# Four small reorderings in an attention and scan kernel: head loads and maxima on SyncE, the maxima's way out of PSUM, VectorE's order over the PSUM ring, and the two projection halves

## The chip, the cores and the metric

The kernel runs on one core of a Trainium2 chip. The metric is the device time of one execution in microseconds. The kernel before takes 8861.15 us, the median of 3 runs (8851.8 to 8868.71).

## What is computed

The input x has shape (8, 32, 32, 192). Four layers follow one another, each added to its input after a group norm without parameters (`_gn`, 32 groups over the image):

```
x = x + L0(_gn(x))   # A: attention, 12 heads of 16 over 1024 tokens, rope on q and k
x = x + L1(_gn(x))   # B: depthwise 3x3 convolution and a selective scan in 4 directions
x = x + L2(_gn(x))   # C: attention with relative position bias rel_h + rel_w
x = x + L3(_gn(x))   # D: neighbourhood attention, window 7x7, no bias
attn = softmax(q @ k * scale (+ bias)); out = (attn @ v) @ proj (+ b)
```

## The kernel before

The kernel calls the layers A, B, C, D. B (`scan_*`) is a stage of its own. A, C and D share the functions `attn_tensor`, `attn_scalar`, `attn_vector`, `attn_pool` and `attn_sync`, one program for each engine (PE, ACT, DVE, POOL and SP, which issues all DMAs). Each engine works strictly in the order of its program, and they meet at semaphores.

**Turns.** A layer is a row of turns n. A turn does one step of scores and one step of weights, `LEAD` turns apart. A head takes `STEPS` turns, 8 in A and C (one 128-row tile against 1024 keys each) and 4 in D (two tiles of 320 keys each). So an image of 12 heads has 96 turns in A and C and 48 in D, and the lead is 13, 13 and 8.

- `scores(n)`: PE multiplies a query tile with all keys; DVE takes the row maximum (L927) into `mx`.
- `maxima(h)`: after a head's last scores PE transposes `mx` (L681). DVE's `negated` reads the transposed 8x128 tile from PSUM and splits -max into two fp32r parts in D (`nm`, L936, L938) and three bf16 parts in A and C (`nb`, L941 to L947). SP copies them as extra rows into the head's queries (`maxima` in `attn_sync`, L1100), so that the second product comes out with the maximum subtracted. These rows serve the first weights unit of that head.
- `weights(g)`: PE multiplies a key tile with all queries (L694, L698, L700), and ACT takes the exponential (L825) into `pt`.
- `values`: PE multiplies `pt` with v into `px` (L724); ACT and DVE take it out (`outputs`, L832, L954) into `os`; SP's `store` moves it to `dn` and `ocm` (L1115, L1118).

**The ring.** All PSUM results but values go through a ring of 3 slots of 1024 columns. `ring(L)` lists the units in PE's order: in a turn first the planned ones ("sums", "job", "rot", "tokens", "proj"), then the relatives (C alone), scores, maxima, weights. Unit i has slot i % 3. `claim` makes PE wait until unit i - 3 has been read. A maxima unit counts as read when `negated` has ended (`a.nm`).

**The plan.** `agenda(L)` puts the rest of the work at fixed turns: the norm's statistics and sums, four jobs for each image (projections to q and k in halves of 96 channels, with the split into parts, L768 to L903 and SP's `part`, L1065), rot and turn (rope, A alone), tokens (v), the reciprocals of the sums and their spreading (`back`, L1123, `spread`, L1134, POOL's `normal`), the two halves of the output projection (`proj`; PE L631, DVE `residual`, L970, L972) and "leave" (store the image, load the one after next, L388, L382). The two proj halves of an image stand in successive turns, leave one turn later. In D these are turns 20, 21 and 22 of the next image.

**Loads.** A head's q and k parts come from DRAM into one of 4 buffers (`load` in `attn_sync`, L1088, 384 KB a head). For k, a part is read with a repeated (broadcast) outer dimension. In D the load of head h + 3 is issued in the first turn of head h, as seen from scores, and needed in the first turn of the next head. It waits for the parts in DRAM (`s.stored`) and until the buffer's last weights step has run (`s.st_ps`). In that turn of D SP does the planned work, then `maxima`, then `load`; `store` of a head comes two turns later.

**DVE's turn** is scores(n) first, then the planned work in plan order, then relatives, negated, outputs.

Of the kernel before, what the change touches and what calls it, by code (L numbers as in the profile page):

```python
# [7 lines left out]
F32 = mybir.dt.float32  # L8
F32R = mybir.dt.float32r
BF16 = mybir.dt.bfloat16  # L10
ALU = mybir.AluOpType
# [3 lines left out]
B, H, W, C = 8, 32, 32, 192  # L15
N = H * W
NH, HD = 12, 16
CP = 96
NC = C // CP
# [109 lines left out]
class HeadSignals:  # L129
    def __init__(self, sem):  # L130
        self.qk_ps = sem("qk_ps")
        self.top = sem("top")
        self.low = sem("low")
        self.v_ps = sem("v_ps")
        self.v_used = sem("v_used")
        self.mt = sem("mt")
        self.nm = sem("nm")
        self.odd = sem("odd")
        self.os = sem("os")
        self.o_in = [sem(f"o_in{i}") for i in range(2)]  # L140
        self.rdn = sem("rdn")
        self.rd_out = sem("rd_out")
        self.rb_in = sem("rb_in")
        self.oc = [sem(f"oc{i}") for i in range(NC)]
        self.proj_ps = sem("proj_ps")
# [219 lines left out]
def turns(L, img):  # L365

    return B * LAYERS.index(L) + img
# [39 lines left out]
def norm_variance(nc, dve, m, sums, turn):  # L407
    dve.wait_ge(m.i.stat_sums, turn + 1)
    nc.vector.tensor_copy(m.gs[:], sums.rearrange("p (c s) -> p c s", c=NC)).then_inc(m.i.sums_used, 1)
    nc.vector.drain()  # L410
    nc.vector.tensor_tensor(m.gt[:], m.gs[:, :, 0], m.gs[:, :, 0], ALU.mult)
    nc.vector.drain()
    nc.vector.tensor_tensor(m.gv[:], m.gs[:, :, 1], m.gt[:], ALU.subtract).then_inc(m.i.var, 1)
# [52 lines left out]
def agenda(L):  # L466

    plan = {}

    def put(n, kind, img, i=0):  # L470
        plan.setdefault(n, []).append((kind, img, i))

    size, lead = per_image(L), LEAD[L]
    ahead, behind = AHEAD[L], BEHIND[L]
    for img in range(B):
        start = size * (img - 1)
        for c in range(NC):
            put(start + ahead["norm"] + c, "statistics", img, c)
        put(start + ahead["norm"] + 1, "moments", img)
        put(start + ahead["norm"] + 3, "sums", img)  # L480
        put(start + ahead["norm"] + 4, "apply", img)
        for i, n in enumerate(ahead["jobs"]):
            for kind, lag in JOB_LAGS[L].items():
                put(start + n + lag, kind, img, i)
        for i, n in enumerate(ahead["tokens"]):
            put(start + n, "tokens", img, i)
        for c, end in ((0, size * img + lead + 7 * STEPS[L] - behind["reciprocal"]), (1, size * (img + 1))):
            for kind in ("reciprocal", "back", "spread", "normal"):
                put(end + behind[kind], kind, img, c)
        for c in range(NC):  # L490
            put(size * (img + 1) + behind["proj"] + c, "proj", img, c)
        put(size * (img + 1) + behind["proj"] + 2, "leave", img)
    return plan


def turns_of(L, plan):

    return range(min(plan), max(plan) + 1)
# [18 lines left out]
def maxima_ready(L, n):  # L517

    return n % STEPS[L] == 0 and 0 < n <= per_image(L) * B
# [31 lines left out]
def attn_tensor(nc, pe, m, L):  # L551
# [8 lines left out]
    def claim(unit):  # L560

        i = place[unit]
        if i >= SLOTS:
            old = units[i - SLOTS]
            if old[0] == "scores":
                pe.wait_ge(s.mx_used, old[1] + 1)
            elif old[0] == "weights":
                pe.wait_ge(s.pt, old[1] + 1)
            elif old[0] == "maxima":
                pe.wait_ge(a.nm, heads + old[1] + 1)  # L570
            elif old[0] == "relative":
                pe.wait_ge(s.rq, 2 * old[1] + old[2] + 1)
            elif old[0] == "sums":
                pe.wait_ge(m.i.sums_used, turns(L, old[1]) + 1)
            elif old[0] == "tokens":
                pe.wait_ge(a.v_used, 2 * (images + old[1]) + old[2] + 1)
            elif old[0] == "rot":
                pe.wait_ge(s.turned, 4 * old[1] + old[2] + 1)
            elif old[0] == "proj":
                pe.wait_ge(m.i.x_done, NC * turns(L, old[1]) + old[2] + 1)  # L580
            elif L == "A":
                pe.wait_ge(s.raw, 4 * old[1] + old[2] + 1)
            elif L == "C":
                pe.wait_ge(s.rest, 4 * old[1] + old[2] + 1)
            else:
                pe.wait_ge(a.low, 4 * (images + old[1]) + old[2] + 1)
        return m.ring[:, i % SLOTS, :]
# [267 lines left out]
def attn_vector(nc, dve, m, L):  # L855
# [14 lines left out]

    def turn(img, i):

        dve.wait_ge(s.rot_ps, 4 * img + i + 1)
        nc.vector.tensor_tensor(m.rs[:], m.ring[0:CP, slot[("rot", img, i)], :], m.sin[:], ALU.mult) \
            .then_inc(s.turned, 1)
# [53 lines left out]
    def negated(h):  # L929

        dve.wait_ge(a.mt, heads + h + 1)
        if h >= 1:
            dve.wait_ge(s.nm_in, MAX_IN[L] * h)
        mt = m.ring[0:NT, slot[("maxima", h)], 0:P]
        if L == "D":
            nc.vector.tensor_scalar(m.nm[:, 0, :], mt, -1.0, None, ALU.mult)  # L936
            nc.vector.drain()
            nc.vector.scalar_tensor_tensor(m.nm[:, 1, :], mt, -1.0, m.nm[:, 0, :].bitcast(F32),  # L938
                                           ALU.mult, ALU.subtract).then_inc(a.nm, 1)
        else:  # L940
            nc.vector.tensor_scalar(m.nb[:, 0, :], mt, -1.0, None, ALU.mult)  # L941
            nc.vector.drain()
            nc.vector.scalar_tensor_tensor(m.nr[:], mt, -1.0, m.nb[:, 0, :], ALU.mult, ALU.subtract)
            nc.vector.drain()
            nc.vector.tensor_copy(m.nb[:, 1, :], m.nr[:])
            nc.vector.drain()
            nc.vector.tensor_tensor(m.nb[:, 2, :], m.nr[:], m.nb[:, 1, :], ALU.subtract).then_inc(a.nm, 1)  # L947
# [24 lines left out]
            nc.vector.tensor_tensor(x, psum, x, ALU.add).then_inc(m.i.x_done, 1)  # L972

    for n in turns_of(L, plan):
        if 0 <= n < total:
            scores(n)
        for kind, img, i in plan.get(n, []):
            if kind == "statistics":
                if i == 0:
                    dve.wait_ge(m.i.x_in, 16 * (turns(L, img) + 1))  # L980
                norm_statistics(nc, m, m.x[img % 2], i)
            if kind == "moments":
                norm_moments(nc, m, turns(L, img))
            if kind == "sums":
                norm_variance(nc, dve, m, m.ring[0:CP, slot[(kind, img, i)], 0:2 * NC], turns(L, img))
            if kind == "apply":
                if img:
                    dve.wait_ge(a.v_ps, 2 * (images + img))
                norm_apply(nc, dve, m, m.x[img % 2], turns(L, img))
            if kind == "turn":  # L990
                turn(img, i)
            if kind == "sum":
                total_of(img, i)
            if kind == "rest":
                rest(img, i)
            if kind == "low":
                low(img, i)
            if kind == "reciprocal":
                reciprocal(img, i)
            if kind == "proj":  # L1000
                residual(img, i)
        for h, axis in relatives(L, n):
            relative(h, axis)
        if maxima_ready(L, n):
            negated(n // steps - 1)
        g = n - lead
        if g % steps == 2 and steps < g <= total + 2:
            outputs(g // steps - 1)
# [31 lines left out]
def attn_sync(nc, sp, m, L, x_from, x_to, d):  # L1040
    s, a = m.s[L], m.a
# [95 lines left out]
    for n in turns_of(L, plan):  # L1137
        for kind, img, i in plan.get(n, []):
            if kind == "part":
                part(img, i)  # L1140
                jobs += 1
                if img == 0 and i == 1:
                    for h in range(NBUF):
                        load(h, jobs)
            if kind == "back":
                back(img, i)
            if kind == "spread":
                spread(img, i)
            if kind == "leave":
                store_image(sp, m, L, img, x_to)  # L1150
                if img + 2 < B:
                    load_image(sp, m, L, img + 2, x_from)
        if maxima_ready(L, n):
            maxima(n // steps - 1)
        h, left = divmod(n - lead, steps)
        if left == 0 and 1 <= h and h - 1 + NBUF < NH * B:
            sp.wait_ge(s.st_ps, steps * h)
            load(h - 1 + NBUF, jobs)
        if left == 2 and 1 <= h <= NH * B:
            store(h - 1)  # L1160

# [579 lines left out]
```

## Time and profile before

| | before |
|---|---|
| median of 3 runs | 8861.15 us |
| profiled execution | 8870.59 us |
| its span | 8868.8 us |
| PE busy | 7117.3 us, 80% |
| DVE busy | 5281.6 us, 60% |
| ACT busy | 3280.4 us, 37% |
| granted TensorE clock, mean | 0.864 |
| stage A / B / C / D, about | 50 to 1880 / 4562 / 7410 / 8869 us |

Times within the profile are microseconds from the start of the span. A clock of 1.00 is TensorE at 2.4 GHz, 0.50 at 1.2 GHz. "PE" is the matmul, "PEld" the weight load, "SPq" what SP's sequencer issues. An arrow `<-` in a wait names who released it. L numbers are lines of the kernel before. The profiled execution is 9.4 us over the median of the runs.

### The profile page before, as it was taken

Reading aid. Unit: us, or ns where it says so; the run is one execution under the profiler, and the core shown is the slowest. Engines: PE = TensorE matmul, PEld = TensorE weight load, DVE = VectorE, ACT = ScalarE, POOL = GpSimd, SP = SyncE. Lnnn points to the kernel's source line nnn. Section 1 sums busy time; section 2 is a strip of 40 time slices with the busy share of each in tenths; the row PEclk is TensorE's granted clock in tenths of the full one; section 3 lists DMA queues with packets and bytes.
Section 4 is the critical chain, followed back from the end, with each engine's and each line's share of the span. In section 5 each row is a group of like instructions: output and inputs, shape, how many; then the busy total and the mean of one; then the engine's idle time right before and its main releaser. Section 6 shows DMA issues by size and latency. Waiting matters only on the chain. (4 is left out here: it accounts for less than half of the span.)

```text
span 8868.8 us, 86314 instructions
## 1 busy us (share of the span) xinstructions
PE 7117.3 (80%) x32664; PEld 2841.9 (32%) x32664; DVE 5281.6 (60%) x5310; ACT 3280.4 (37%) x3610; POOL 1168.2 (13%) x468
## 2 busy tenths in 40 slices
PE   6888888867777777777779999999989996777776
PEld 2222222223223223233234343344333432333332
DVE  5777777757777767777765555555555553333333
ACT  2555555532323322322323343333433432222222
POOL 0000000014334334334320000000000000000000
PEclk9999999988878778778778999999989997888787
DMA  2111111100000000000001001111010101222221
GB/s 65 47 46 48 48 48 48 46 23 0 7 7 0 7 7 0 7 7 0 4 29 29 27 29 35 29 30 30 27 35 27 30 25 54 65 66 62 64 68 46
DMA packets 152812, 282.83 MB, mean 32 GB/s; under 512 B 46858, under 2 KB 53762, under 8 KB 152398
## 3 DMA queue, kind: packets, MB, share of 16 engines
q1 hardware_dynamic: 152398, 277.31, 10.8%
q8 instruction: 260, 4.26, 0.2%
q14 instruction: 154, 1.26, 0.0%
HBM read 165.34 MB, written 89.79 MB: 29 GB/s over the span
## 5 line engine op out<-in xcount | busy, mean ns | idle before, releaser
L927 DVE TENSOR_REDUCE mx<-ring 128x1 f32<-128x1024 f32 (+1 forms) x1920 | 2187.8, 1141 | 2536.0 <-PE ring L674 1255.0
L825 ACT ACTIVATE pt<-ring 128x1024 f32<-128x1024 f32 (+1 forms) x1920 | 1868.4, 981 | 2836.0 <-PE ring L700 1329.5
L724 PE MATMUL px<-pt,vo 128*32 128x512 f32 (+3 forms) x8064 | 1277.2, 616 | 9.5 <-ACT pt L825 9.3
L671 PE MATMUL ring<-kb,qb 96*128 96x512 bf16 x3072 | 1121.2, 407 | 203.0 <-DVE rq L912 96.2
L698 PE MATMUL ring<-qb,kb 99*128 99x512 bf16 x3072 | 1124.0, 408 | 161.7 <-DVE nb L947 67.9
L1533 POOL TENSOR_TENSOR hc<-hs,crep 128x1024 f32<-128x1024 f32 x384 | 979.7, 2551 | 1684.0 <-DVE hs L1489 1593.7
L1228 PE MATMUL ring<-duh,spread 96*128 96x512 f32 x1536 | 650.7, 537 | 362.0 <-DVE hs L1478 230.5
L1489 DVE TENSOR_TENSOR_SCAN hs<-ring,hs 128x1024 f32<-128x1024 f32 x384 | 874.5, 2277 | 2.1 <-ACT ring L1376 2.1
L700 PE MATMUL ring<-rq,hot 128*128 128x512 f32 x1536 | 865.5, 622 | 0.0
L674 PE MATMUL ring<-hot,rq 128*128 128x512 f32 x1536 | 856.6, 616 | 0.0
L1376 ACT ACTIVATE ring<-ring,arow 128x1024 f32<-128x1024 f32 x384 | 415.9, 1083 | 947.8 <-PE ring L1217 947.8
L698 PEld LDWEIGHTS ring<-qb,kb 99*128 99x128 bf16 x3072 | 266.7, 100 | 1319.9 <-issue 684.5
L1478 DVE TENSOR_TENSOR hs<-ring,brep 128x1024 f32<-128x1024 f32 x384 | 467.3, 1217 | 358.8 <-PE ring L1228 312.6
L671 PEld LDWEIGHTS ring<-kb,qb 96*128 96x128 bf16 x3072 | 280.7, 100 | 907.0 <-issue 396.5
L1217 PE MATMUL ring<-dth,spread 96*128 96x512 f32 x1536 | 521.1, 467 | 30.4 <-DVE hs L1489 29.6
L667 PE MATMUL ring<-ks,qs 112*128 112x320 f32 x768 | 270.4, 441 | 330.5 <-DMA ks<-qk_split 295.2
L1228 PEld LDWEIGHTS ring<-duh,spread 96*128 96x128 f32 x1536 | 307.3, 218 | 699.8 <-DVE hs L1478 298.8
L1243 PE MATMUL px<-hc,fold 128*32 128x512 f32 x1536 | 476.0, 1018 | 31.8 <-POOL hc L1533 30.9
L1217 PEld LDWEIGHTS ring<-dth,spread 96*128 96x128 f32 x1536 | 313.4, 221 | 480.6 <-issue 346.4
L1030 POOL TENSOR_TENSOR ocn<-ocm,rb 96x1024 f32<-96x1024 f32 x24 | 56.7, 2362 | 2717.1 <-DMA rb<-reciprocals 2388.0
L1030 POOL TENSOR_TENSOR ocm<-ocm,rb 96x1024 f32<-96x1024 f32 x24 | 56.4, 2351 | 2428.2 <-DMA rb<-reciprocals 2428.2
L667 PEld LDWEIGHTS ring<-ks,qs 112*128 112x128 f32 x768 | 147.2, 234 | 609.5 <-issue 505.4
(169 smaller groups left out, 6792.5 us busy)
## 6 DMA issues: line engine op xcount, KB each, us to landing
qk_parts<-part SPq DMA_DIRECT2D x192, 192.0 KB, 2.4
qb<-qk_parts SPq DMA_DIRECT2D x192, 96.0 KB
kb<-qk_parts SPq DMA_DIRECT2D x192, 96.0 KB
ocm<-os SPq DMA_DIRECT2D x576, 32.0 KB
rb<-reciprocals SPq DMA_DIRECT2D x288, 64.0 KB, 2.5
qb<-qk_parts SPq DMA_DIRECT2D x192, 64.0 KB
kb<-qk_parts SPq DMA_DIRECT2D x192, 64.0 KB
qk_split<-hi SPq DMA_DIRECT2D x32, 384.0 KB, 3.5
```

What stands on the lines that cost most here:

```text
L671: last = nc.tensor.matmul(out[:, half], m.qb[u][0:BR, q], m.kb[u][0:BR, half], start=True, stop=L == "A")
L674: last = nc.tensor.matmul(out[:, half], m.rq[u][:, q], m.hot[:, half], start=False, stop=True)
L698: last = nc.tensor.matmul(out[:, half], m.kb[u][:, k], m.qb[u][:, half], start=True, stop=L == "A")
L700: last = nc.tensor.matmul(out[:, half], m.hot[:, k], m.rq[u][:, half], start=False, stop=True)
L724: last = nc.tensor.matmul(m.px[32 * g:32 * g + 32, h % 2, lo - f * HF:hi - f * HF], m.vo[img % 2][:, t, VW * head:VW * head + VC], pt[:, l ...
L825: nc.scalar.activation(pt, ps, ACT.Exp, scale=1.0 if L == "C" else HD ** -0.5).then_inc(s.pt, 1)
L927: nc.vector.tensor_reduce(out, ps, AX.X, ALU.max).then_inc(s.mx_used, 1)
L1217: last = nc.tensor.matmul(m.s2[:, i % 2, f * HF:(f + 1) * HF], m.spread[:, ORDER[j], :], m.dth[k % 2][:, part, f * HF:(f + 1) * HF], start ...
L1228: last = nc.tensor.matmul(m.s1[:, f, :], m.spread[:, ORDER[j], :], m.duh[k % 2][:, part, f * HF:(f + 1) * HF], start=part == 0, stop=part ...
L1243: last = nc.tensor.matmul(m.px[32 * band:32 * (band + 1), f, :], m.fold[:, v, :], rhs, start=False, stop=t >= TILES - BANDS, skip_group_ch ...
L1489: nc.vector.tensor_tensor_scan(m.hs[i % HSS][:], m.s2[:, i % 2, :], m.hs[i % HSS][:], 0.0, ALU.mult, ALU.add).then_inc(s.h, 1)
L1533: nc.gpsimd.tensor_tensor(m.hc[i % HCS][:], m.hs[i % HSS][:], m.crep[k % 2][:], ALU.mult).then_inc(s.hc, 1)
```

## The change

- In `attn_sync`, `load` comes before `maxima` within a turn.
- `negated` takes the transposed maxima out of PSUM with its first operation, into `nr`, and signals `mt_used`; the parts are then made from `nr`. PE's claim after a maxima unit waits for `mt_used`. D has three operations instead of two, A and C five instead of four.
- DVE does the plan's "sums", "turn", "proj", "rest" (in C) and "low" (in D) ahead of scores(n), in PE's order. `turn` also waits for the sum of the job before.
- The second proj half stands two turns after the first, and leave one turn later than before (three after the first half).

```diff
+        self.mt_used = sem("mt_used")
...
         for c in range(NC):
-            put(size * (img + 1) + behind["proj"] + c, "proj", img, c)
-        put(size * (img + 1) + behind["proj"] + 2, "leave", img)
+            put(size * (img + 1) + behind["proj"] + 2 * c, "proj", img, c)
+        put(size * (img + 1) + behind["proj"] + 3, "leave", img)
...
             elif old[0] == "maxima":
-                pe.wait_ge(a.nm, heads + old[1] + 1)
+                pe.wait_ge(a.mt_used, heads + old[1] + 1)
...
     def turn(img, i):
+        if 4 * img + i:
+            dve.wait_ge(s.rotated, 4 * img + i)
         dve.wait_ge(s.rot_ps, 4 * img + i + 1)
...
         mt = m.ring[0:NT, slot[("maxima", h)], 0:P]
+        nc.vector.tensor_scalar(m.nr[:], mt, -1.0, None, ALU.mult).then_inc(a.mt_used, 1)
+        nc.vector.drain()
         if L == "D":
-            nc.vector.tensor_scalar(m.nm[:, 0, :], mt, -1.0, None, ALU.mult)
+            nc.vector.tensor_copy(m.nm[:, 0, :], m.nr[:])
             nc.vector.drain()
-            nc.vector.scalar_tensor_tensor(m.nm[:, 1, :], mt, -1.0, m.nm[:, 0, :].bitcast(F32),
-                                           ALU.mult, ALU.subtract).then_inc(a.nm, 1)
+            nc.vector.tensor_tensor(m.nm[:, 1, :], m.nr[:], m.nm[:, 0, :].bitcast(F32), ALU.subtract).then_inc(a.nm, 1)
         else:
-            nc.vector.tensor_scalar(m.nb[:, 0, :], mt, -1.0, None, ALU.mult)
+            nc.vector.tensor_copy(m.nb[:, 0, :], m.nr[:])
             nc.vector.drain()
-            nc.vector.scalar_tensor_tensor(m.nr[:], mt, -1.0, m.nb[:, 0, :], ALU.mult, ALU.subtract)
+            nc.vector.tensor_tensor(m.nr[:], m.nr[:], m.nb[:, 0, :], ALU.subtract)
...
     for n in turns_of(L, plan):
+        for kind, img, i in plan.get(n, []):
+            if kind == "sums":
+                norm_variance(...)
+            if kind == "turn":
+                turn(img, i)
+            if kind == "rest" and L == "C":
+                rest(img, i)
+            if kind == "low" and L == "D":
+                low(img, i)
+            if kind == "proj":
+                residual(img, i)
         if 0 <= n < total:
             scores(n)
         for kind, img, i in plan.get(n, []):
...
-            if kind == "rest":
+            if kind == "rest" and L == "A":
                 rest(img, i)
-            if kind == "low":
+            if kind == "low" and L != "D":
                 low(img, i)
...
# attn_sync
-        if maxima_ready(L, n):
-            maxima(n // steps - 1)
         h, left = divmod(n - lead, steps)
         if left == 0 and 1 <= h and h - 1 + NBUF < NH * B:
             sp.wait_ge(s.st_ps, steps * h)
             load(h - 1 + NBUF, jobs)
+        if maxima_ready(L, n):
+            maxima(n // steps - 1)
         if left == 2 and 1 <= h <= NH * B:
             store(h - 1)
```

## Rows read from the trace of the kernel before

**Rows 1.** Stages A, C, D: length, busy PE, PEld, DVE, ACT, POOL; clock; DMA; GB/s.

```profile
50.00:1880.00 1830.00, 1541.75 (x7024) 438.96 (x7024) 1295.96 (x1514) 941.68 (x1008) 112.72 (x48) 0.94 0.16 46
...
4562.00:7410.00 2848.00, 2563.73 (x16112) 1123.85 (x16112) 1479.03 (x1646) 1110.29 (x1168) 37.81 (x16) 0.91 0.10 30
7410.00:8868.80 1458.80, 1051.79 (x4208) 472.40 (x4208) 530.23 (x842) 415.11 (x560) 37.78 (x16) 0.79 0.22 64
```

**Rows 2.** PE's waits in stage D: releaser, us in total, times, longest.

```profile
PE ring L667 <- DMA ks<-qk_split: 295.2, 67, 8.1
...
PE ring L694 <- DVE x L972: 12.8, 7, 1.8
```

**Rows 3.** The timeline of one plain head in D: start, us, engine, operation.

```profile
7802.12 0.53 PE L667 MATMUL ring<-ks,qs 112*128 112x320 f32 x2 [3.03 <-DMA ks<-qk_split]
...
7804.08 1.38 SPq L1100 DMA_DIRECT2D qs<-nm  x2
...
7805.57 1.11 SPq L1088 DMA_DIRECT2D qs<-qk_split  x2
...
7806.90 0.56 PE L667 MATMUL ring<-ks,qs 112*128 112x320 f32 x2
...
7808.94 1.29 SPq L1115 DMA_DIRECT2D dn<-os  x2
...
7810.28 1.18 SPq L1118 DMA_DIRECT2D ocm<-os  x2
7814.15 0.87 PE L667 MATMUL ring<-ks,qs 112*128 112x320 f32 x2 [3.95 <-DMA ks<-qk_split]
```

**Rows 4.** The waits of SP's queue in stage D.

```profile
SPq L1100 <- DVE nm L938: 390.0, 75, 11.7
...
SPq L1134 <- DMA reciprocals<-rdn: 50.9, 16, 6.0
...
SPq L381 <- DMA out<-x: 23.8, 6, 4.0
```

**Rows 5.** The timeline of a head in D that starts without a stall.

```profile
7871.20 0.56 PE L667 MATMUL ring<-ks,qs 112*128 112x320 f32 x2
...
7875.88 0.67 DVE L954 TENSOR_TENSOR os<-px,odd 64x512 f32<-64x512 f32 x1
...
7876.14 0.56 PE L667 MATMUL ring<-ks,qs 112*128 112x320 f32 x2
```

**Rows 6.** Two half-microsecond windows of the plain head, columns as in rows 1.

```profile
7803.50:7804.00 0.50, 0.50 (x4) 0.00 (x0) 0.43 (x3) 0.50 (x1) 0.00 (x0) 0.50 0.00 0
...
7810.50:7811.00 0.50, 0.00 (x0) 0.00 (x0) 0.00 (x0) 0.00 (x0) 0.00 (x0) 1.00 0.15 59
```

**Rows 7.** PE's waits in stage A.

```profile
PE ring L698 <- DVE nb L947: 62.0, 84, 2.1
...
PE ring L671 <- DVE rs L874: 27.6, 21, 2.7
...
PE ring L671 <- DVE gs L409: 4.1, 7, 0.9
```

**Rows 8.** PE's waits in stage C.

```profile
PE ring L698 <- DVE raw L891: 20.4, 14, 1.5
...
PE ring L671 <- DVE x L970: 4.3, 7, 0.6
```

**Rows 9.** The timeline of a job's reading in C.

```profile
5459.67 1.11 ACT L768 ACTIVATE part<-ring,qk_bC 96x1024 bf16<-96x1024 f32 x1 [2.47 <-PE ring L597]
...
5461.65 1.27 DVE L891 SCALAR_TENSOR_TENSOR raw<-ring,qk_bC,part 96x1024 f32<-96x1024 f32 x1
...
5462.98 0.39 PE L698 MATMUL ring<-qb,kb 99*128 99x512 bf16 x1 [1.40 <-DVE raw L891]
```

**Rows 10.** The timeline of the maxima in A.

```profile
1006.72 0.27 DVE L941 TENSOR_SCALAR nb<-ring 8x128 bf16<-8x128 f32 x1
...
1008.04 0.60 PE L698 MATMUL ring<-qb,kb 99*128 99x512 bf16 x2 [0.58 <-DVE nb L947]
```

More of the change, by code:

```diff
@@ L974, in attn_vector @@
     for n in turns_of(L, plan):
+        for kind, img, i in plan.get(n, []):
+            if kind == "sums":
+                norm_variance(nc, dve, m, m.ring[0:CP, slot[(kind, img, i)], 0:2 * NC], turns(L, img))
+            if kind == "turn":
[6 more added lines that the diff above has]
+                residual(img, i)
         if 0 <= n < total:
@@ L983, in attn_vector @@
                 norm_moments(nc, m, turns(L, img))
-            if kind == "sums":
-                norm_variance(nc, dve, m, m.ring[0:CP, slot[(kind, img, i)], 0:2 * NC], turns(L, img))
             if kind == "apply":
@@ L989, in attn_vector @@
                 norm_apply(nc, dve, m, m.x[img % 2], turns(L, img))
-            if kind == "turn":
-                turn(img, i)
             if kind == "sum":
                 total_of(img, i)
-            if kind == "rest":
+            if kind == "rest" and L == "A":
                 rest(img, i)
-            if kind == "low":
+            if kind == "low" and L != "D":
                 low(img, i)
@@ L999, in attn_vector @@
                 reciprocal(img, i)
-            if kind == "proj":
-                residual(img, i)
         for h, axis in relatives(L, n):
```

## The prediction

> **What bounds the kernel now.** I read the span by stages first, then who waited for whom in each, then the order of time around the longest wait.
>
> The stage table [rows 1] shows TensorE (PE) busy for 84% of stage A, 90% of C and 72% of D, while DVE is at 71%, 52% and 36%. PE sets the pace in all three, and its idle time is what this change can reach: 288 us in A, 284 us in C, 407 us in D. Stage B is not touched. The low clock is a second cost: the granted clock averages 0.79 in D against 0.91 and 0.94.
>
> In D one wait stands out [rows 2]: 67 times PE waits for a head's qs/ks rows, 295.2 us in all, 4.4 us each.
>
> Why those rows are late is seen in the order of time around one plain head [rows 3]. Its first scores start at 7802.12. The SP queue, which issues all DMAs, stands until the DVE has the negated maxima, issues them at 7804.08 (1.38 us), and only then issues the load at 7805.57. The load's user starts at 7814.15. So a load takes 8.6 us from first issue to use, and the period is 3.5 + 8.6 = 12.0 us. SP had been free since the previous store; the queue's own waits [rows 4] put 390.0 us, 75 times, on "DVE nm".
>
> PE alone doesn't need 12 us: a head that starts without a wait has its first, and its fourth turn 4.94 us later [rows 5], so its four turns take 4.94 + 1.61 = 6.55 us, at full clock. After the 4 us of a stall the clock is granted at half, 1.2 GHz [rows 6], and the first two turns take 4.8 us instead of 3.3 [rows 3, 5].
>
> In A and C the waits are short ones for ring slots [rows 7, 8]. In A: 62.0 us for the maxima's slot (84 times), and five rows for slots of rot, proj and sums, from 27.6 to 4.1, together 74.1 us. In C, beside the relatives' slots, which the change leaves alone: six rows for job, proj, sums and maxima, from 20.4 down to 4.3, together 65.5 us.
>
> **The load ahead of the maxima.** In A and C a load's turn is 5 modulo 8 and the maxima's is 0, so the swap changes nothing there. In D both fall on n % 4 = 0. The load's only other waits are for its parts in DRAM and for st_ps of the turn before, which PE has passed when the head starts. It is then issued as soon as the store of turn n - 2 is out of SP's queue.
>
> The new chain: in a full-clock head, os starts 4.68 us and ends 5.35 us after the head's start [rows 5]; dn and ocm take SP 1.29 + 1.18 us, with gaps 2.5 us [rows 3]; so SP is free at 7.9 us. The load issued then is used 8.6 us later, at 16.5 us, and its user is the head after next. So the period is 16.5 / 2 = 8.3 us, 1.7 us over PE's 6.55. The stall doesn't vanish, it falls from 4.4 to about 1.7 us. If each stall still brings the half clock for two turns (+1.5 us, os later by up to 1.5 us) the period is 9.6 us. I take 8.8.
>
> Sum for D: 67 waits x (4.4 - 1.7) = 181 us. Clock: 1.5 us x 67 = 100 us if all of it came back; half, 50 us, since 1.7 us of idleness stays in each head. Together 231 us. Checked by the period: 67 x (12.0 - 8.8) = 214 us. Ends: PE alone, 67 x (12.0 - 6.55) = 365 us; and 80 us, where the stall still costs 3.2 us a head because the maxima or SP's queue are late in the load's place.
>
> What moves behind the load: the maxima's two issues. SP has them out 2.3 us (four load issues) + 1.4 us after the load's start. They are needed one scores unit after the load is, since both serve turn n + 4. But they sit behind 384 KB. The trace shows what this means. Between 7810.5 and 7811.0 the DMA share is 0.15 with 59 GB/s moved [rows 6]: the tail of the load is on two of 16 engines, for some 4 us. And a small DMA (reciprocals, 24 KB) issued behind a load kept the queue waiting for up to 6.0 us [rows 4]. So the maxima land with the load's tail, not before it. I cost that at nothing: cover is that weights come after scores and the transpose, 0.6 us. Without cover it is that lateness, 67 times.
>
> By the Trainium skill ("DMA: Bandwidth & Descriptors", Queues, rings and completion order; and on how many engines) a DMA is split over the largest k up to 16 that divides its slowest dimension, always on the lowest-numbered engines, and each engine takes descriptors in ring order. The ks load with its broadcast outer 2 would be on engines 0 and 1 and the 8-row maxima on 0 to 7, so the maxima would stand behind the load on two engines. By that rule the trace's two busy engines agree, and it makes the first rival below.
>
> **Leave one turn later, proj two units apart.** Image stores and loads (SP, plan turn 22 of 48 in D) move to turn 23. SP stands some 4.0 us for the image's store before it issues the next load [rows 4], now directly ahead of the head load of turn 24, and the 768 KB image load is now directly ahead of it in the DMA queues; before, a store and the maxima lay between. Once per image, about 3 us: 8 x 3 = -24 us in D. In A and C loads have slack (PE waited for kb once in each, at the start), nothing. The spacing itself removes the DVE's two residuals back to back; with the reorder D's proj waits go, 12.8 us [rows 2] and a second row of half that. Net in D about 231 - 24 + 19 = 226, rounded to 225 us.
>
> **DVE in ring order.** PE fills plan units before scores(n), but DVE reduced scores(n) first. In C [rows 9] a job's part is ready at 5460.78 (5459.67 + 1.11), DVE does the reduction of 1.23 us first, then rest, and PE's weights start at 5462.98, 1.40 us late. After: rest 5460.8 to 5462.1, weights 0.9 us earlier; scores(n)'s reduction ends at 5463.3 instead of 5461.7, and scores(n + 1) may wait 0.3 us for it. Such a stall goes by two thirds. proj and sums go whole, since their data is ready when PE ends. The relatives keep their place after scores(n), so their waits stay. C: 65.5 us x 0.75 = 50 us (20 to 90, the upper end with clock regained after the 2 us stalls).
> In A the same: 74.1 us. DVE is the busier engine there, and each operation that comes first makes scores(n) later by 1.2 us, which the next weights unit claims. Half: 37 us. The wait for s.rotated that turn gains is for DVE's own sum of two turns earlier; nothing. In D low can't start before ACT's hi, which ends when the reduction does: nothing.
>
> **Maxima by one operation.** In A the slot was held by four operations from 1006.72 on, and PE's weights started at 1008.04, 0.58 us late [rows 10]. Now it is free after the first, 0.27 us. But the chain is one operation longer, a cast of 0.21 us and a drain of 0.07 to 0.13: the two reductions that stand behind it end 0.3 us later, and the third weights unit after the maxima claims the second one's slot. By the rows it then starts only 0.1 us earlier, though units after it can regain 0.3. I take 0.25 of 0.58: 96 x 0.25 = 24 us (-20 to 60). C and D have slack on DVE: nothing but the 5.9 us counted above. The nm for SP is 0.3 us later, and SP has the load to issue in that time.
>
> **Sum.** D 225, C 50, A 37 + 24 = 61: 336 us. The profiled execution took 8870.6 us (span 8868.8): 8870.6 - 336 = 8534.6. The median shown is 9.4 us under the profiled one: 8525.
>
> **Rivals.**
> 1. PE waits in D for the maxima or for SP's queue in the load's place. For: [rows 4, 6]. Against: the load itself ends at the same moment. If the maxima land 2 us after it, D gives 67 x 2 = 134 us less: 91 + 111 = 202 us, 8660.
> 2. A and C give nothing, as DVE turns each freed slot into a late reduction. For: A's two reductions back to back behind the maxima; against: C's DVE idles half the time. D alone: 8861 - 225 = 8636.
> 3. Slower: the maxima come so late behind the load that they set D's period. Place: weights of turn n + 4; they also hold DVE, whose next negated waits for nm_in. From 12.0 - 8.3 = 3.7 us behind the load D gains nothing; at 3.7 + 111 / 67 = 5.4 us the whole is even; at 8 us it is 8861 + 67 x 4.3 - 111 = 9038. Against: behind the last load descriptor only 4 KB per row remain.
> 4. The clock comes back in full and stalls shrink with it (PE near 6.9 us a head): D 340, C 70, A 61: 8390 or so.
>
> Chances: the forecast 0.62, rival 1 0.11, rival 2 0.14, rival 4 0.10, rival 3 0.03. The range, 8430 to 8690, takes in rivals 1 and 2 and half of 4. What a measurement can tell from no change is 0.2%, 18 us. Faster than that 0.95, within it 0.02, slower 0.03.
>
> **What would show it.** In the changed profile: in D, heads without jobs 8.3 to 9.6 us apart, the ks wait near 1.7 us a time, "DVE nm" as SP's wait cut to a fraction, and D's clock above 0.85 (if it stays at 0.79, the clock half fails). No wait for "nb" in A's PE rows, but some for "mx". C's waits for rq as before, those for raw, x and gs under 20 us. Wrong would be: a PE wait for qs<-nm in dozens (rival 1), A's 61 us missing (rival 2), or D's heads still over 11 us apart.

## The result and the profile after

The changed kernel takes 8531.05 us, the median of 4 runs (8513.62 to 8533.49), against 8864.93 us for the kernel before on the same chip: ratio 0.9624, 95% interval 0.961 to 0.9638. Forecast was 8525, in the range 8430 to 8690. The profiled execution has a span of 8531.7 us. The sum was right by luck: two errors cancel in it.

The stage table after, first A, C and D, columns as in [rows 1] (B, between A and C, is 2680 us in both):

```profile
40.00:1770.00 1730.00, 1513.85 (x7024) 425.02 (x7024) 1313.84 (x1617) 942.59 (x1008) 113.03 (x48) 0.97 0.17 49
...
4453.00:7226.00 2773.00, 2531.36 (x16112) 1127.13 (x16112) 1496.46 (x1742) 1110.40 (x1168) 37.97 (x16) 0.92 0.11 31
7226.00:8531.70 1305.70, 983.37 (x4208) 446.19 (x4208) 546.30 (x938) 415.29 (x560) 37.73 (x16) 0.84 0.24 71
```

Taken between the first image loads of the stages, the change by stage is:

```
          before    after   measured   forecast
A         1839.5   1730.0    -109.5       -61
B         2681.3   2680.4      -0.9         0
C         2848.3   2773.4     -74.9       -50
D         1456.4   1305.5    -150.9      -225
```

PE's waits after, in A, where [rows 7] stood:

```profile
PE ring L672 <- ACT pt L826: 35.0, 140, 0.3
PE ring L699 <- DMA qb<-nb: 21.6, 13, 2.6
PE ring L682 <- DVE mx L930: 18.5, 23, 1.3
PE ring L672 <- DVE mx L930: 14.6, 10, 8.2
...
PE ring L699 <- DVE mx L930: 12.0, 19, 1.1
PE ring L672 <- DVE x L974: 7.1, 14, 0.5
...
PE ring L699 <- DVE nr L938: 6.1, 10, 0.7
```

The rows for mx in A before:

```profile
PE ring L671 <- DVE mx L927: 12.3, 8, 7.1
...
PE ring L681 <- DVE mx L927: 11.4, 9, 1.3
...
PE ring L698 <- DVE mx L927: 3.5, 8, 1.3
```

In C the two long rows for the relatives, before:

```profile
PE ring L671 <- DVE rq L912: 96.2, 77, 2.5
PE ring L648 <- DVE rq L912: 54.7, 78, 1.7
```

After, in C, where [rows 8] stood, then in D, where [rows 2] stood:

```profile
PE ring L672 <- DVE rq L915: 113.2, 84, 2.5
PE ring L649 <- DVE rq L915: 60.9, 79, 1.7
...
PE ring L699 <- DVE raw L894: 4.0, 7, 0.6
```

```profile
PE ring L668 <- DMA ks<-qk_split: 226.4, 49, 13.5
PE ring L668 <- DVE lo L902: 21.2, 21, 1.0
...
PE ring L695 <- DVE nr L938: 0.9, 3, 0.4
PE ring L695 <- DVE x L976: 0.2, 1, 0.2
```

What the reader is to see: the maxima's 62.0 us in A (was nb) is 6.1 us for nr. The five rows for rot, proj and sums, 74.1 us, are down to 7.1 us for x, but the rows for mx grew from 27.2 to 45.1 us. C's 20.4 us for raw is 4.0, while the relatives' rows (all that wait for rq) grew from 177.5 to 196.2 us. D has 49 ks waits instead of 67, but they are longer, 4.6 us a time and up to 13.5. Counted by the head that they stand ahead of, 16 of the 67 waits and 106 of the 295 us were those of heads 7 and 10 of an image; now these are 16 of the 49, and 129 of the 226 us. Among the plain heads the wait ahead of heads 1 and 3 is gone (but for the first image), and the one ahead of heads 0 and 2 is 2.2 to 4.0 us. SP's queue in D, where [rows 4] stood:

```profile
SPq L1124 <- DVE os L958: 184.7, 66, 8.6
SPq L1109 <- DVE nm L943: 169.1, 49, 11.7
...
SPq L1082 <- DMA qk_split<-lo: 29.6, 8, 4.3
...
SPq L382 <- DMA out<-x: 24.4, 6, 4.4
```

"DVE nm" fell from 390.0 to 169.1 us. The wait for the parts just written (qk_split<-lo) is 29.6 us, and was less than half of that before:

```profile
SPq L1073 <- DMA qk_split<-lo: 12.9, 8, 3.6
```

Two plain heads of D after, where [rows 3] stood:

```profile
7888.52 1.13 SPq L1097 DMA_DIRECT2D qs<-qk_split  x2
...
7890.45 0.53 PE L668 MATMUL ring<-ks,qs 112*128 112x320 f32 x2 [3.32 <-DMA ks<-qk_split]
...
7897.29 1.28 SPq L1124 DMA_DIRECT2D dn<-os  x2
...
7898.47 0.55 PE L668 MATMUL ring<-ks,qs 112*128 112x320 f32 x2
...
7899.91 1.62 SPq L1097 DMA_DIRECT2D qs<-qk_split  x2
...
7908.56 0.87 PE L668 MATMUL ring<-ks,qs 112*128 112x320 f32 x2 [3.48 <-DMA ks<-qk_split]
```

The load is issued when the store's issues end, is used 8.6 us later (7899.91 to 7908.56), and the two heads together take 18.1 us: one of 8.0 without a stall, one of 10.1 with one. The forecast chain said 8.3 to 9.6 us a head.

The whole of D and A, head by head, shows what each part does. Each number is the time from a head's first scores to the next one's, mean of images 1 to 6, worked out from the starts of the scores matmuls; s1 to s4 are the four parts alone on the kernel before, u, v and w variants of the changed kernel (below). A plain head is one without planned work:

```
D, head        0    1    2    3    4    5    6    7    8    9   10   11   sum
before       12.6 12.2 12.3 12.3 15.7 17.0 14.1 16.4 17.8 20.0 13.3 12.2  175.9
s1 load       8.3  9.9  8.8  9.9 14.6 16.2 13.9 16.3 17.7 19.9 13.3 10.3  159.2
s2 one op    12.7 12.4 12.4 12.6 15.5 17.1 14.1 15.6 17.0 19.9 13.4 12.4  175.2
s3 order     12.3 12.0 12.2 12.2 15.6 14.5 13.7 16.0 16.4 19.9 14.2 12.1  171.2
s4 spacing   12.4 11.9 12.2 12.0 15.4 15.4 18.3 16.6 16.9 19.9 13.7 12.0  176.8
after         8.0 10.1  9.3  9.8 14.5 12.1 19.2 14.7 17.8 20.0 14.2 10.0  159.7
u2 image      8.4  9.9  8.1  9.9 14.5 11.3 15.2 19.1 17.9 19.8 13.2  9.8  157.1
u3 parts      8.4  9.9  8.7  9.7 14.8 11.6 19.1 15.6 17.5 17.9 14.3  9.8  157.4
u5 16 rows    6.9  7.3  7.4  7.4 11.6 11.0 15.0 16.1 17.7 15.8 12.8  7.1  136.2
u6 maxima    12.5 12.5 12.4 12.4 15.3 12.4 17.9 16.6 17.0 20.0 14.2 12.5  175.7
w1 no spac.   8.2 10.1  8.2 10.0 14.6 11.5 13.1 16.6 17.3 19.9 13.5  9.8  152.9
v3           7.2  7.3  7.2  7.3 11.4 11.3  6.6 22.5 17.6 14.6 11.7  7.1  131.8
A, head
before       13.9 13.9 13.9 24.9 14.8 22.4 26.4 26.3 21.7 17.6 13.9 13.9  223.5
s2 one op    13.4 13.4 13.5 26.6 14.6 22.6 26.4 26.5 19.2 16.6 13.5 13.4  219.8
s3 order     13.9 13.9 13.9 22.8 14.1 20.2 22.9 25.6 18.6 16.4 13.9 13.9  209.8
after        13.4 13.4 13.4 20.0 17.7 21.0 22.8 25.4 17.3 16.7 13.4 13.5  207.9
```

### The profile page after: what moved, and what is told of

Its sections match the earlier page's. It is cut to its first block and busy times, and to the rows that moved or that the text cites. A ratio compares the mean times of both kernels' runs of the same rounds, so it can differ in the third digit from the quotient of the medians.

```text
span 8531.7 us, 86921 instructions
## 1 busy us (share of the span) xinstructions
PE 6989.7 (82%) x32664; PEld 2806.6 (33%) x32664; DVE 5325.8 (62%) x5598; ACT 3281.8 (38%) x3610; POOL 1169.1 (14%) x468
## 5 line engine op out<-in xcount | busy, mean ns | idle before, releaser
L725 PE MATMUL px<-pt,vo 128*32 128x512 f32 (+3 forms) x8064 | 1232.0, 599 | 7.6 <-ACT pt L826 7.5
L699 PE MATMUL ring<-qb,kb 99*128 99x512 bf16 x3072 | 1102.0, 400 | 49.6 <-DMA qb<-nb 21.6
L668 PE MATMUL ring<-ks,qs 112*128 112x320 f32 x768 | 255.4, 420 | 255.2 <-DMA ks<-qk_split 226.4
L675 PEld LDWEIGHTS ring<-hot,rq 128*128 128x128 f32 x1536 | 327.1, 213 | 10.9 <-issue 10.3
```

Of the source, the lines that this page charges most:

```text
L675: last = nc.tensor.matmul(out[:, half], m.rq[u][:, q], m.hot[:, half], start=False, stop=True)
L699: last = nc.tensor.matmul(out[:, half], m.kb[u][:, k], m.qb[u][:, half], start=True, stop=L == "A")
L725: last = nc.tensor.matmul(m.px[32 * g:32 * g + 32, h % 2, lo - f * HF:hi - f * HF], m.vo[img % 2][:, t, VW * head:VW * head + VC], pt[:, l ...
```

## The experiments

All ratios are to the kernel before on the same chip. Stage times are those of one profile each; B, which no kernel here touches, lies between 2668 and 2682 us in them, so a difference under 10 us says nothing.

Totals and stage times don't quite agree. The profile of the kernel before is of an execution of 8870.59 us, while its median was 8839.0 to 8844.7 us on the chips of all experiments. So stage differences to it add up to some 26 to 32 us more than the totals give, and which stage holds them is not shown. D is hardly the place: s2, which does nothing for D's pace, has D at 1451.8 us on another chip, against 1456.4.

### The four parts, each alone

**s1, the load first.** The two lines go from ahead of SP's head load to behind it.

```diff
-        if maxima_ready(L, n):
-            maxima(n // steps - 1)
...
+        if maxima_ready(L, n):
+            maxima(n // steps - 1)
```

> The kernel before with the head load ahead of the maxima alone. My theory: only D moves. Stage D falls from 1456 us to about 1300, heads without planned work 8.0 to 10 us apart; A stays at 1839 within 5 us, C at 2848, B at 2681. Total about -150 us, ratio 0.983. Rival (part of D's gain came from VectorE's order and the early slot): D falls by under 110 us here.

8724.28 us, ratio 0.9868 (0.9848 to 0.9887). D 1304.0 us, C 2844.9, A 1849.7. The gain is in D, -152 us, nearly all of it in the heads without planned work (12.3 to 8.3 and 9.9 us); heads 4 and 5 give 1.9 us an image, heads 6 to 10 don't move. The total gives less, 117 us (100 to 135). By D's stage time, on which it was stated, the rival is out. The two terms of the forecast can be read apart here. The ks waits fell from 295.2 us by 97:

```profile
PE ring L667 <- DMA ks<-qk_split: 198.2, 48, 7.8
```

And PE's busy time in D fell from 1051.79 us by 55, for the same 4208 matmuls:

```profile
7420.00:8724.00 1304.00, 996.60 (x4208) 451.41 (x4208) 530.05 (x842) 414.67 (x560) 37.78 (x16) 0.83 0.24 71
```

Together that is the 152 us.

**s2, the maxima by one operation** (the `negated` and `mt_used` lines of the diff above).

> The kernel before with the maxima taken out of PSUM by one operation alone. My theory: A gains 0.5 us for each of 96 heads, so about -48 us, C -6, D 0 (the load sets its pace): ratio 0.994. Rival, the forecast's own pricing (DVE's longer chain takes half back): A -24 us, ratio 0.997.

8820.85 us, ratio 0.9979 (0.997 to 0.9989). A 1807.1 us (-32), its plain heads 13.9 to 13.4 us; C 2837.0, D 1451.8. The plain heads give the 0.5 us that I expected, twice the forecast's 0.25, but head 3 gives 1.7 back. In A the wait for the maxima's slot fell from 62.0 to 3.9 us and the stage by 32 only: the waits for qb<-nb rose from 12.1 to 20.9 us and PE's busy time by 9. The total gives 19 us (10 to 27), nearer to the rival's 24 than to my 54.

**s3, DVE in ring order** (the `attn_vector` loop and `turn` of the diff above).

> The kernel before with VectorE's new order alone. My theory: A and C gain in the heads with jobs alone, A -35 to -50 us, C -50 us, D within 15 us: ratio 0.989. Rival (the reductions that now stand behind the planned work take it all back): within 20 us of before.

8670.73 us, ratio 0.9815 (0.98 to 0.9829): the largest part. A 1745.2 us (-94), C 2799.1 (-49), D 1414.1 (-42). I was too low in A and missed D. The stage table of A and D in it has the clock up in both:

```profile
40.00:1785.00 1745.00, 1503.27 (x7024) 430.49 (x7024) 1298.33 (x1520) 940.64 (x1008) 112.96 (x48) 0.97 0.16 49
...
7257.00:8670.70 1413.70, 1037.61 (x4208) 466.43 (x4208) 526.55 (x842) 414.76 (x560) 37.72 (x16) 0.81 0.22 66
```

In A the granted clock rises from 0.94 to 0.97 and PE's busy time falls by 38 us, though it does the same matmuls; its idle time between the same marks falls by 47. The slot waits [rows 7] are worth 74 us by themselves, so a part of them came back as other waits: the rows for mx are 36.8 us instead of 27.2, and x has 3.6. s1, s2 and s4 have 0.94 to 0.95 still, so the clock came with this part. The total gives 164 us (152 to 177) where the three stages give 185.

**s4, the projection halves two turns apart** (the two `put` lines).

> The kernel before with the two projection halves two turns apart and leave one turn later, alone. My theory: A -10 to -20 us, C -15 us, D +5 to +20 us since the image's store and load now stand ahead of a head load: ratio 0.997. Rival (spacing is worth nothing once it stands alone, because DVE still reduces scores first): all stages within 5 us.

8867.74 us, ratio 1.0035 (1.0022 to 1.0048): slower by a third of a per cent. Per image, A and C are even: A's heads 3 and 4 take 40.9 us together instead of 39.7. In D head 6 goes from 14.1 to 18.3 us and head 5 from 17.0 to 15.4. Spacing alone buys nothing. By stage nothing is lost either (A 1840.6, C 2843.6, D 1455.7 us), and this profile is of its fastest execution, so where the third of a per cent goes is not shown.

### Parts taken out of the changed kernel

**u6, the maxima first again** (s1's edit reversed).

> The changed kernel, with the maxima ahead of the head load again. My theory: A and C as in the changed kernel (1730 and 2773 us), D between 1400 and 1425 us, where VectorE's order alone left it: ratio 0.974 to 0.978. Rival (the load's place is worth less once the other three parts are in, since D then waits for leave and parts): D under 1370 us, ratio under 0.971.

8680.06 us, ratio 0.9816 (0.9801 to 0.9831). D 1451.0 us, A 1730.4, C 2780.3. So the load's place is worth 145.5 us in D with the other parts in, as alone; both numbers I gave were off, because D stands at 1451 without it and not at 1414. Head 6 has most of that, 17.9 us against 13.7 in s3, which has no spacing. The plain heads show a part too: 12.5 us against 12.2 in s3, since with the maxima first the longer chain (0.3 us) stands ahead of the load. The ratios of u6 and the changed kernel are 170 us apart, so more than D shows.

**w1, the halves in successive turns** (leave again in the turn after the second half).

```diff
-            put(size * (img + 1) + behind["proj"] + 2 * c, "proj", img, c)
-        put(size * (img + 1) + behind["proj"] + 3, "leave", img)
+            put(size * (img + 1) + behind["proj"] + c, "proj", img, c)
+        put(size * (img + 1) + behind["proj"] + 2, "leave", img)
```

> The changed kernel with the two projection halves in successive turns and leave one turn later, as before: the first three parts of the change alone. My theory (spacing is worth nothing in A and C and delays the head load behind the image load in D): D's heads 5 and 6 fall from 31.3 to about 28 us, A and C within 8 us, total 20 to 30 us under the changed kernel; ratio 0.960. Rival (with VectorE in ring order the spacing pays, since DVE's residual and reduction no longer stand back to back): 10 us or more over the changed kernel.

8483.6 us, ratio 0.9596 (0.9582 to 0.961). D 1257.5 us, 48 under the changed kernel, A and C within 4 us of it. Head 6 of D goes from 19.2 to 13.1 us. So the fourth part costs 48 us by D's profile. The totals say less: 25 us between the ratios, and 39 against u4, which is the changed kernel but for the maxima's chain and ran on the same chip. The forecast's 24 is at the low end. Without the spacing the parts simply add up in D: 1456.4 less the 152.4 of s1, the 4.6 of s2 and the 42.3 of s3 is 1257.1 us. Why the spacing is worth nothing in D alone (s4) and costs 48 us here is shown in part only: it costs head 6 of an image 4.2 us there and 6.1 here, and the 1.6 us that it gave back in head 5 there it does not give here (11.5 us in w1, 12.1 in the changed kernel).

**u4, the slot released by the second operation** of the old, shorter chain.

```diff
-        nc.vector.tensor_scalar(m.nr[:], mt, -1.0, None, ALU.mult).then_inc(a.mt_used, 1)
-        nc.vector.drain()
...
+            nc.vector.tensor_scalar(m.nb[:, 0, :], mt, -1.0, None, ALU.mult)
+            nc.vector.drain()
+            nc.vector.scalar_tensor_tensor(m.nr[:], mt, -1.0, m.nb[:, 0, :], ALU.mult, ALU.subtract) \
+                .then_inc(a.mt_used, 1)
```

> The changed kernel with the old, shorter maxima chain (four operations in A and C, two in D); the ring slot is released after the second operation, the last that reads PSUM. My theory (in A's plain heads the slot's release is what counted and the longer chain costs nothing there; in D the chain stands ahead of SP's maxima only): A's plain heads stay at 13.4 us within 0.1, D within 10 us of the changed kernel's 1305; total within 15 us of it, ratio 0.962 to 0.964. Rival (DVE is short in A and the extra operation costs what the early slot gives): A's plain heads at 13.1 or less, A by 25 us or more.

8522.17 us, ratio 0.9637 (0.9618 to 0.9656), the changed kernel's within the interval. A's plain heads stay at 13.4 us, A 1730.6, D 1301.7. So the early release was the gain. A release 0.3 us later and a chain one operation shorter move it no further together; that neither would alone is not shown, since the two could offset each other.

### What holds D now

Head 6 of the changed kernel in order of time:

```profile
7953.40 1.29 SPq L1124 DMA_DIRECT2D dn<-os  x2
...
7954.74 1.18 SPq L1127 DMA_DIRECT2D ocm<-os  x2
...
7955.96 0.57 SPq L389 DMA_DIRECT2D out<-x  x1
...
7960.63 0.32 SPq L383 DMA_DIRECT2D x<-x_C  x1
7961.07 1.14 SPq L1097 DMA_DIRECT2D qs<-qk_split  x2
...
7972.84 0.87 PE L668 MATMUL ring<-ks,qs 112*128 112x320 f32 x2 [12.04 <-DMA ks<-qk_split]
```

SP puts the head's store first, then the image's store, stands 4 us, issues the image load and then the head load. That one is used 11.8 us after its issue instead of 8.6, and PE stands 12.04 us. The same load, the one for head 7, in four kernels, from the starts of SP's issues and of the scores matmul, images 1 to 6:

```
             image load ahead by    issue to use
before              4.4             8.4 to 8.7
w1 no spac.         3.0             8.6 to 10.1
s4 spacing          1.9             9.6 to 10.5
after               0.4            11.5 to 12.9
```

The image's store moves nearer too, from 8.8 us ahead of the head load to 5.0 to 5.6, so the table doesn't tell the two apart.

**u2, the image load behind the head load** in D. It is noted in the queue's turn and issued behind the head load and the maxima.

```diff
             if kind == "leave":
                 store_image(sp, m, L, img, x_to)
-                if img + 2 < B:
+                if L == "D":
+                    coming = img + 2
+                elif img + 2 < B:
                     load_image(sp, m, L, img + 2, x_from)
...
+            if coming < B:
+                load_image(sp, m, L, coming, x_from)
+            coming = B
```

> The changed kernel, with D's image load issued after the next turn's head load and maxima instead of ahead of them. My theory (head 6 of an image takes 19.2 us instead of 14.1 because SP stands for the image's store and then puts 768 KB ahead of the head load): the head load's issue to use falls from 11.7 back to 8.6 us, head 6 to 15 to 16 us, D by 20 to 30 us; ratio to before 0.960. Rival (the 19.2 us come from SP's wait for the store alone, not from the order in the DMA queues): head 6 stays over 18 us.

8513.04 us, ratio 0.9629 (0.9615 to 0.9643); the total can't tell it from the changed kernel. D 1284.8 us in the profile. Head 6 falls to 15.2 us, but not for my reason. The same place in this run:

```profile
7935.73 0.57 SPq L389 DMA_DIRECT2D out<-x  x1
7936.42 2.45 SPq L1097 DMA_DIRECT2D qs<-qk_split  x2
...
7948.83 0.87 PE L668 MATMUL ring<-ks,qs 112*128 112x320 f32 x2 [8.27 <-DMA ks<-qk_split]
```

From issue to use the load takes 12.4 us here, and 12.4 to 13.2 in images 1 to 6: it did not fall. What fell away is the 4 us for which SP stood between the image's store and the head load; the load is issued 0.7 us behind the store instead of 5.1, and the store's 768 KB now stand where the image load's stood. Head 7 rises from 14.7 to 19.1 us. 2.9 of these 4.4 us are PE's busy time, 13.5 to 16.4 us for the same matmuls, at a granted clock of 0.58 instead of 0.76 (mean of images 1 to 6). And DVE, whose statistics need the image, waits longer for it, first in the changed kernel, then here:

```profile
DVE gn L395 <- DMA x<-x_C: 42.2, 7, 7.8
```

```profile
DVE gn L395 <- DMA x<-x_C: 64.8, 7, 11.0
```

Which of the two comes first no run shows.

**u3, a load waits for its own image's parts alone.**

```diff
-            sp.wait_ge(s.stored[i], JOB_OUT[L] * (jobs // 2))
+            sp.wait_ge(s.stored[i], JOB_OUT[L] * (2 * (h // NH) + (2 if h // NH or jobs > 2 else jobs // 2)))
```

> The changed kernel, with a head load waiting only for the parts of its own image, not for all parts issued so far. My theory (in turn 36 the load, now first, waits 4.3 us for a part just issued, which the maxima's issue used to cover): heads 9 and 10 together fall from 34.2 to 30 us, D by about 25 us, SP's wait for qk_split<-lo from 29.6 to under 5 us; ratio 0.960. Rival (heads 9 and 10 are held by PE's jobs, not by that load): D within 8 us of the changed kernel.

8516.6 us, ratio 0.9636 (0.962 to 0.9652). D 1285.0 us; heads 9 and 10 take 32.2 us instead of 34.2, and SP's wait for the parts falls to 6.3 us:

```profile
SPq L1082 <- DMA qk_split<-lo: 6.3, 2, 3.6
```

The mechanism is there, at half the expected 4 us. In total it isn't resolved.

**u5, head loads of D in DMAs of 16 rows.**

```diff
                 if L == "D":
-                    to = to.bitcast(F32)
-                sp.dma_start(to, parts).then_inc(s.heads[u], 16)
+                    for k in range(n):
+                        one = src[h // NH % 2, side, k if side == 0 else p, row:row + HD, :]
+                        sp.dma_start(to[k * HD:(k + 1) * HD, :].bitcast(F32), one).then_inc(s.heads[u], 16)
+                else:
+                    sp.dma_start(to, parts).then_inc(s.heads[u], 16)
```

> The changed kernel, with D's head loads in DMAs of 16 rows with one source row block each (6 for a head instead of 4), so that none has an outer dimension of 2. My theory (the 8.6 us from issue to use are the tail of two DMAs that run on two engines, 32 rows of 159 ns each): issue to use falls to 6 to 7 us, the two plain heads from 18.1 us together to 14 to 15, D by 80 to 110 us; ratio 0.951. Rival (8.6 us is latency and HBM time, and SP's issues are what is scarce): two more issues make heads longer by 1.1 us, D +40 to +80 us.

8344.73 us, ratio 0.9434 (0.9419 to 0.9448). D 1113.7 us, 192 under the changed kernel (168 between the ratios), about twice my number: the plain heads go to 6.9 to 7.4 us, within 0.9 of PE's own 6.55. The ks waits are 82.8 us instead of 226.4. Two windows of a load's tail, the changed kernel's (load issued at 7888.52) and this one's (issued at 7528.85), columns as in [rows 1]:

```profile
7894.50:7895.00 0.50, 0.50 (x5) 0.12 (x4) 0.27 (x1) 0.41 (x1) 0.00 (x0) 1.00 0.15 55
```

```profile
7530.50:7531.00 0.50, 0.50 (x5) 0.50 (x4) 0.00 (x0) 0.47 (x2) 0.00 (x0) 1.00 0.61 189
...
7533.00:7533.50 0.50, 0.50 (x7) 0.08 (x6) 0.50 (x1) 0.46 (x1) 0.00 (x0) 1.00 0.04 8
```

Six microseconds after its issue the old load still crawls at 55 GB/s on 0.15 of the engines. The new one moves 189 GB/s and is over after 4.2 us. Where PE waits for it, it is used 4.6 to 6.1 us after its issue instead of 8.6, ahead of head 7 (images 1 to 6) 7.4 to 8.6 instead of 11.5 to 12.9. By the Trainium skill ("DMA: Bandwidth & Descriptors", on how many engines) an outer dimension of 2 gives two engines. The trace agrees: 0.12 to 0.15 of 16 engines, as in most windows of the old tail, is 1.9 to 2.4 of them. By that rule the qs load would be hit like the ks load, since its source is also two blocks of 16 rows, and the gain agrees with both being cured. The edit also makes six smaller DMAs of four, and no run here has smaller DMAs on the same few engines.

**v2 and v3, a better version.** v2 is the changed kernel with u2, u3, u4 and u5; v3 the same with w1's successive halves.

> The changed kernel with four more edits together: head loads of D in 16-row DMAs, the image load of D behind the head load, a load waits for its own image's parts, and the slot released after the second operation of the shorter chain. If they add up: 8343 of the 16-row loads alone, less 20 for each of the next two, so 8300 us, ratio 0.938. If the 16-row loads have already taken what the other two would give (a load has slack then), within 12 us of 8343.

> The same four edits, and the two projection halves in successive turns as before the change. My theory: the spacing's cost in D was the order of the image load and the head load, which these edits have mended, so it is within 12 us of the kernel with the four edits. Rival (the spacing costs by itself): 20 us or more under it.

v2 8321.49 us, ratio 0.9414 (0.94 to 0.9428), 20 us or so under u5: D 1106.6, so u2, u3 and u4 add 7 us there, as the second reading had it; the total lies between the two readings, and its interval touches that of u5. v3 8289.81 us, ratio 0.9379 (0.9365 to 0.9393), D 1080.5: the spacing costs 26 us in D by itself (32 in the total, on the same chip), against my theory. v3 is the fastest of all. Its clock in D is 0.92 and the load hardly waits:

```profile
7208.00:8288.50 1080.50, 918.66 (x4208) 416.38 (x4208) 525.33 (x842) 414.82 (x560) 37.63 (x16) 0.92 0.31 86
```

```profile
PE ring L671 <- DVE mx L933: 33.2, 8, 6.2
PE ring L671 <- DMA ks<-qk_split: 21.2, 27, 2.4
```

Its longest head is now head 7, 22.5 us.

## Why the prediction was right, and where it was not

**The load ahead of the maxima: mechanism right, size a third too large.** The chain (os, store's issues, load's issue, 8.6 us, the user is the head after next) is what the trace shows, and the plain heads' mean of 9.3 us lies in the 8.3 to 9.6 given. But the plain heads do not stall alike, 1.7 us each: every second one stalls, as 3.32 and 3.48 us in the rows above, which is 1.7 us a head. The sign "ks wait near 1.7 us a time" failed for that reason, and more so through heads 7 and 10, with 4.6. The term mis-sized is "67 waits x (4.4 - 1.7)", 181 us, where s1 measured 97. It gave every wait the plain head's gain. The clock's term, 50 us, was right: 55. In all the part is worth 145 to 152 us by D's profiles, not 231: heads 7 to 10 have jobs and other waits ahead of SP's load, and s1 leaves them as they were (106 us of waits ahead of heads 7 and 10 before, 100 in s1). A count of waits was taken for a count of equal waits; a table by head would have shown 5 or 6 plain heads of 12.

**What stands in the load's way now.** The step "the load's only other waits are for its parts in DRAM and for st_ps" priced the parts at nothing. They were at nothing because the maxima's issue stood between; SP's wait for them is 29.6 us against 12.9 before. u3 got 2 us an image back.

**Maxima behind the load: right.** They land with the load's tail and cost nothing; no new wait for qs<-nm appears in D. Rivals 1 and 3 are out.

**Leave and spacing: sign right, size low.** 24 us were forecast; w1 says 48 by D's profile, 25 to 39 by the totals. The image load ahead of the head load brings 3.2 us of 11.8, as forecast, or the image's store does (u2 has the one without the other, and 12.4). What I left out is that SP now issues the head's store before the image's store, so that the 4 us stand starts later too. The 19 us credited to D's proj waits came from DVE's order, not from the spacing: s3 has neither of the two rows for x, s4 keeps both, at 12.9 and 6.5 us.

**DVE in ring order: the number right in C, too low in A and D.** C -49 alone, 50 forecast, but made up otherwise: in s3 the six slot rows fell from 65.5 to 14.6 us, the relatives' rows rose from 177.5 to 199.1, and PE's busy time fell by 20.5. That the relatives' waits would stay was wrong, and the clock made up for it, so the hit is in part luck. In A I took half of 74.1 us and got 94 measured. Two errors: the reductions that now come later cost 13 us of waits in s3 (mx and x), not 37, and the clock came back, 0.94 to 0.97, where I had put it at nothing. In D I wrote that low gains nothing, which holds (the lo rows are 21.2 us before and after). The 42 us there are the two rows for x, 19 us, 15 us less of ks waits and 14 us less of PE's busy time, with a few us back in small waits.

**Maxima by one operation: within its bounds.** 24 us forecast, 32 measured alone in A and 19 (10 to 27) in the total. About half of the slot's 58 us was taken back, as forecast, but not by the reductions: in s2 the rows for mx are 23.1 us against 27.2, while the waits for qb<-nb, which now come one operation later, and PE's busy time rose by 9 us each. In the plain heads 0.5 of 0.58 us came through, not 0.25. Rival 2 (A and C give nothing) is out by 184 us.

**The clock in D.** The forecast wanted it above 0.85 and it is 0.84, just short; PE's busy time fell by 68 us in the changed kernel. Rival 4 has the clock back in full, and v3, at 0.92 with hardly a ks wait, shows how far 0.84 is from that. So D's 151 us are 68 us of PE's busy time, 69 of ks waits and 19 of waits for x, less 6 in small ones, and the total was hit because D's 74 us too much met 73 us too little in A and C.

## What to carry to other kernels

Where one queue issues all DMAs, look at what stands between a transfer's earliest moment and its issue, and then at what will stand there after the change: each wait that the old order hid behind a longer one comes out. Where a small ring of buffers joins engines, let each engine free the slots in the order in which they are filled, and price the clock with the stall. And look at how many engines a load's tail runs on before its place is moved: cutting the load into DMAs of 16 rows was worth 192 us in D here, the load's new place 145 to 152.

## What the runs showed of the hardware

- A head load of 384 KB in four DMAs took 8.2 to 9.4 us from issue to use where PE waited for it, mostly 8.6, leaving out the first image and the loads that follow an image's transfer; most of its tail ran at 0.12 to 0.15 of the DMA engines. In six DMAs of 16 rows it took 4.6 to 6.1 us (u5).
- With 768 KB issued 0.4 us ahead of it (an image load) the four-DMA load took 11.5 to 12.9 us, with 768 KB issued 0.7 us ahead (an image's store) 12.4 to 13.2, and with an image load 4.4 us ahead 8.4 to 8.7.
- PE's busy time for the same matmuls follows the granted clock: the 7024 of A took 1541.75 us at a mean of 0.94 and 1503.27 at 0.97 (s3), and those of head 7 in D, from image to image of the changed kernel, 11.7 us at 0.87 to 18.7 at 0.50.
